# The table of expert groups in three pieces among the products of the last shared expert

## What is computed

```
x = x + layernorm(attention_block(layernorm(x)))
x = x + layernorm(experts(layernorm(x)))

# experts, E = 8 routed experts of inner width I = 176, top 2, shared expert of inner width SI = 704
shared  = (silu(x @ sw_gate) * (x @ sw_up)) @ sw_down
probs   = softmax(x @ router_w.T)
top_w, top_i = top_k(probs, 2);  top_w = top_w / sum(top_w)
h       = silu(x @ w_gate[e]) * (x @ w_up[e])          # for each expert e
routed  = sum over e of (h @ w_down[e]) * weight of e for the token
out     = routed + sigmoid(x @ shared_gate_w) * shared
```

## Time and profile before

| | us |
|---|---|
| median of 3 runs | 630.02 (627.61 to 630.73) |
| the profiled execution | 628.59 |
| its span, from the first to the last instruction | 626.9 |
| TensorE busy | 532.7 (85%) |
| VectorE busy | 413.1 (66%) |
| ScalarE busy | 259.0 (41%) |
| GpSimd busy | 110.3 (18%) |
| mean granted clock of TensorE | 0.922 |

### The profile page before, as it was taken

How to read it: one execution, slowest core, us unless ns; L and a number is a source line. 1 busy time by engine, 2 the same in 40 slices (tenths; PEclk the granted TensorE clock), 3 DMA queues, 4 the chain that set the end, 5 groups by cost and what they waited for, 6 DMA issues and landing times.

```text
span 626.9 us, 8174 instructions
## 1 busy us (share of the span) xinstructions
PE 532.7 (85%) x2464; PEld 421.3 (67%) x2464; DVE 413.1 (66%) x1249; ACT 259.0 (41%) x463; POOL 110.3 (18%) x133
## 2 busy tenths in 40 slices
PE   2835359999658999999989998999996989999991
PEld 1413235587437677787758886888784889999870
DVE  6786643779874698885488684333647747667447
ACT  3711344524355424357431444311232546666404
POOL 1510001300001404001205000031005014444400
PEclk9986678999767999999989999799987989999997
DMA  8970000001010003002001000010007214444273
GB/s 288 425 189 11 23 2 0 0 1 35 28 40 1 0 2 102 1 34 68 1 0 51 19 35 34 2 42 27 33 2 269 52 41 123 136 121 121 81 264 134
DMA packets 29549, 44.42 MB, mean 71 GB/s; under 512 B 3211, under 2 KB 24203, under 8 KB 29163
## 3 DMA queue, kind: packets, MB, share of 16 engines
q1 hardware_dynamic: 24515, 32.95, 16.4%
q0 software_dynamic: 3408, 9.38, 4.0%
q10 hardware_dynamic: 1584, 1.57, 0.8%
HBM read 27.55 MB, written 16.34 MB: 70 GB/s over the span
## 4 chain that ended last, share of the span: by engine, by line
PE 55%; DVE 33%; ACT 6%; issue 3%; DMA 2%; POOL 0%; ACTq 0%; POOLq 0%; DVEq 0%; SPq 0%
PE psum L723 10%; PE psum L764 10%; PE psum L724 10%; PE psum L725 9%; PE psum L790 5%; PE psum L733 3%; PE psum L839 3%; DVE rt L999 2%; DVE rt L1000 2%; DVE SM L1322 2%; PE psum L931 1%; DVE XC L1196 1%; PE psum L914 1%; PE psum L825 1%; PE psum L961 1%
## 5 line engine op out<-in xcount | busy, mean ns | idle before, releaser
L633 ACT ACTIVATE SM<-psum 128x512 f32<-128x512 f32 (+1 forms) x56 | 33.1, 595 | 132.0 <-PE psum L725 106.5
L1322 DVE TENSOR_TENSOR SM<-SM,psum 128x512 f32<-128x512 f32 (+1 forms) x56 | 38.1, 683 | 60.1 <-ACT SM L633 59.9
L509 POOL DMA_INDIRECT x_dispatched<-XN,dest x32 | 33.4, 1044 | 164.9 <-DVE XN L1390 156.3
L764 PE MATMUL psum<-WOU,SM 128*128 128x256 f32 x256 | 60.2, 379 | 0.2 <-DVE SM L1322 0.2
L790 PE MATMUL psum<-WQKV,HT 128*128 128x512 f32 (+1 forms) x128 | 51.1, 552 | 6.8 <-ACT GA L620 3.3
L500 POOL TENSOR_TENSOR OG<-QKV,hvec 128x256 f32<-128x256 f32 x16 | 13.3, 834 | 244.5 <-ACT IG L575 225.4
L764 PEld LDWEIGHTS psum<-WOU,SM 128*128 128x128 f32 x256 | 48.1, 189 | 9.2 <-issue 1.0
L518 POOL DMA_INDIRECT y_routed<-GO,g_dest x39 | 37.8, 969 | 70.1 <-ACT GO L698 69.8
L790 PEld LDWEIGHTS psum<-WQKV,HT 128*128 128x128 f32 x128 | 26.6, 213 | 29.7 <-issue 25.0
L764 PE MATMUL psum<-SDN,SM 128*128 128x256 f32 (+1 forms) x192 | 46.4, 392 | 0.1
L764 PEld LDWEIGHTS psum<-SDN,SM 128*128 128x128 f32 (+1 forms) x192 | 36.9, 195 | 7.7 <-issue 1.3
(11 more groups left out here) (285 smaller groups left out, 1357.1 us busy)
## 6 DMA issues: line engine op xcount, KB each, us to landing
XG<-x_dispatched SPq DMA_DIRECT2D x39, 130.0 KB, 2.6
YF<-y_routed SPq DMA_DIRECT2D x4, 1024.0 KB, 8.9
RUPR<-rup SPq DMA_DIRECT2D x1, 2816.0 KB
X<-x SPq DMA_DIRECT2D x4, 512.0 KB, 6.4
x_after_attention<-X SPq DMA_DIRECT2D x4, 512.0 KB, 2.8
QKV<-x ACTq DMA_DIRECT2D x3, 512.0 KB, 3.6
y_shared<-SH SPq DMA_DIRECT2D x3, 512.0 KB, 2.9
SHF<-y_shared SPq DMA_DIRECT2D x1, 1536.0 KB, 11.0
```

Of the source, the lines that this page charges most:

```text
L509: nc.gpsimd.indirect_dma_start(XD[:, :], bass.IndirectOffsetOnAxis(dest[:, i, old + j:old + j + 1], 0), XN[:, j, :], None).then_inc(dispat ...
L633: nc.scalar.activation(SM[0:rows, g % 3, 0:tb], p_pair(n)[0][0:rows, 0:tb], ACT.Silu).then_inc(silu_ready, 1)
L764: last = nc.tensor.matmul(p_down[:, j // 2, (j % 2) * D:(j % 2 + 1) * D], SM[0:rows, g % 3, j * P:(j + 1) * P], weight[0:rows, m, :], star ...
L1322: nc.vector.tensor_tensor(SM[0:rows, g % 3, 0:tb], SM[0:rows, g % 3, 0:tb], value_rows(n, rows)[:, 0:tb], ALU.mult).then_inc(hid_ready, 1)
```

## The change

The table gets steps of its own in the list, in three pieces: `("table", 3, 0)`, the limits of the experts (seven instructions, with a wait for the last of them added behind), `("table", 3, 1)`, the rows of the groups (L1140 to L1153, up to `table_ready`), and `("table", 3, 2)`, the spare rows (L1155 to L1160). The first two stand behind chunk 0 (`hid` 3,0), the third behind chunk 1 (`hid` 3,1) with `rsplit` 0. The other `rsplit` steps follow: 1 and 2 behind chunk 2, 3 and 4 behind chunk 3, 5 and 6 behind chunk 4, 7 behind chunk 5. GpSimd's row in `PLACE` is changed only in places that belong to steps in which GpSimd does nothing.

```diff
-    pieces = {1: [0, 1], 2: [2, 3], 3: [4, 5], 4: [6, 7]}
-    return order + weave(shared(b), {i: [("rsplit", b, m) for m in ms] for i, ms in pieces.items()})
+    tail = {0: [("table", b, 0), ("table", b, 1)], 1: [("table", b, 2), ("rsplit", b, 0)], 2: [("rsplit", b, 1), ("rsplit", b, 2)],
+            3: [("rsplit", b, 3), ("rsplit", b, 4)], 4: [("rsplit", b, 5), ("rsplit", b, 6)], 5: [("rsplit", b, 7)]}
+    return order + weave(shared(b), tail)
...
-            def table():
+            def per_slot(ap):
+                return ap.unsqueeze(1).broadcast_to([P, NG, E])
+            def table(m):
+                if m == 0:
+                    dve.wait_ge(hid_ready, SLOT[("rank", NB - 1, 0)] + 1)
+                    expert_limits()
+                if m == 1:
+                    group_rows()
+                if m == 2:
+                    spare_rows()
+            def expert_limits():
                 step(nc.vector.tensor_tensor(ntile_i[:, :], base[:, NB, :], base0[:, :], ALU.subtract))
...
                 step(nc.vector.tensor_tensor(jump[:, 1, :], lim[:, 1:E + 1], lim[:, 0:E], ALU.subtract))
-                def per_slot(ap):
-                    return ap.unsqueeze(1).broadcast_to([P, NG, E])
+                settle()
+            def group_rows():
                 link(nc.vector.tensor_tensor(past[:, :, :], slot_i[:, :].unsqueeze(2).broadcast_to([P, NG, E]), per_slot(ends[:, :]),
...
                 nc.vector.tensor_scalar(g_exp[:, :], g_exp[:, :], -1.0, float(E), ALU.mult, ALU.add).then_inc(table_ready, 1)
+            def spare_rows():
                 step(nc.vector.tensor_tensor(g_keep[:, :], g_row[:, :], g_lim[:, :], ALU.subtract))
...
                     nc.vector.reciprocal(gate[:, b % 2, 0:nj], top[:, 0, 0:nj]).then_inc(shared_gate, 1)
-                    if b == NB - 1:
-                        settle()
-                        dve.wait_ge(hid_ready, SLOT[("rank", b, 0)] + 1)
-                        table()
+                if stage == "table":
+                    settle()
+                    table(m)
```

## The result

The changed kernel takes 622.61 us in the median of four runs (621.20 to 623.98) against 629.96 before: ratio 0.9889, 95% interval 0.9851 to 0.9928. Two later sets of runs gave 0.9891 (0.9869 to 0.9912) and 0.9877 (0.9855 to 0.9899). The profiled execution took 623.98 us.

What follows compares the result with a forecast made beforehand. VectorE's queue order was taken as the bound: the table held up the product TensorE waited for. Terms 3.30 + 2.14 - 1.70 = 3.74 us off the median 630.02 gave 626.3 us; range 623.4 to 628.5.

Steps and rivals of the forecast that it cites:

- The stall: TensorE's wait for VectorE's product in the last shared expert: 5.85 us becomes 2.55, saving 3.30 us.
- The splits: VectorE's eight weight splits, moved later in the last shared expert: cost 0, with margins of 1.2 to 2.0 us.
- The other waiters: Group loads on SyncE's queue and GpSimd's scatters: scatters unchanged, first load still issued at about 486.5, cost 0.
- C: Rival: VectorE's splits become the bound ahead of the first group; at twice their length 635.7 us; chance 0.03.
- D: Rival: `hid` 3,2 waits for something other than product 0, so gain 0, 630.0 us; chance 0.03.
- A sign that came true by luck: TensorE's first transposes of a group at about 499 instead of 502.80, or at 497 if the clock stays up.
- case A: Rival: the clock stays up through the shorter stall before `hid` 3,3; gain 5.44 us, 624.6 us; chance 0.20.
- The old stall's clock: TensorE's half-speed stretch of 4.7 us at the stall before `hid` 3,2: 2.14 us lost, now saved.
- The new stall's clock: One half-speed stretch of 3.4 us at the shorter gap before `hid` 3,3: 1.70 us lost, 0 as other end.
- The entry to the groups: TensorE's 1.89 us gap before 505.35, ahead of the experts' groups: stays, with its slow stretch, so no gain.

Runs made afterwards that it cites:

- splits_only: Against the kernel before: only the splits moved back (one, two, two, two, one), the table left whole ahead of product 0; 629.73 us, ratio 1.0004.
- table_only: Against the changed kernel: splits put back two each behind chunks 1 to 4, so only the table is moved; 622.64 us, ratio 0.9892.
- one_piece_each: Against the changed kernel: one table piece behind each of `hid` 3,0, 3,1 and 3,2, the splits rearranged behind chunks 2 to 5; 624.11 us, ratio 0.9917.
- shift_4: Against the changed kernel: four dense products added on TensorE ahead of the last `rank`, pushing the stage back 0.93 us; 625.97 us, ratio 0.9947.
- shift_12: Against the changed kernel: twelve dense products added on TensorE ahead of the last `rank`, pushing the stage back 2.8 us; 628.41 us, ratio 0.9974.
- early_splits: Against the changed kernel: one table piece behind each of `hid` 3,0 to 3,2, splits 0 and 1 in VectorE's earlier wait; 621.84 us, ratio 0.9873.
- early_copies: Against early_splits: ScalarE's gate products of the last `shout` issued behind its first two copies of groups; 618.62 us, ratio 0.9817.
- whole_behind_0: Against the changed kernel: all three table pieces behind `hid` 3,0, ahead of product 1; 627.35 us, ratio 0.9966.
- after_again: The changed kernel itself, unaltered, with a second profile and five more rounds; 622.54 us, ratio 0.9891.
- after_third: The changed kernel itself, unaltered, profiled and timed again beside three others on the same chip; 622.01 us, ratio 0.9877.

## Why the prediction was wrong

*The stall.* It was right in place and size: 5.68 to 2.32 us, 3.36 saved where 3.30 was worked out. Limits, group rows and product 1 started 0.58, 1.85 and 5.96 us behind product 0, where the working had 0.60, 1.85 and 5.96. The limits with their added wait took 1.27 us for 1.25 worked out.

*The splits.* Right: cost 0, shown by splits_only and table_only. The margins that were worked out, 1.2 us for product 5 and 2.0 for split 7, are there in VectorE's timeline of the changed kernel:

```profile
495.67 0.69 DVE L1340 TENSOR_TENSOR SM<-SM,psum 64x512 f32<-64x512 f32 x1
496.28 1.22 DVE L1231 TENSOR_TENSOR RDNL<-RDNR,RDNH 88x1024 fp32r<-88x1024 f32 x1
```

Product 5 ended at 496.36, and `sdn` 3,5 began at about 497.7 (an estimate: eight products of 0.225 us ahead of 499.51); split 7 ended at 497.50, TensorE's products at 499.51. That these are small is what one_piece_each showed, with TensorE 2.3 us earlier.

*The other waiters.* One thing that was to show the prediction wrong did occur: the loads of the groups were issued later. The first came at 490.76, 19.9 us behind `hid` 3,0 where 17.8 was the distance before, behind GpSimd's last scatter issue, which took 2.96 us. The prediction had the scatters unchanged. It cost nothing, since TensorE's first group stood only at 499.51, and no row of TensorE's has a wait for a load there. C and D didn't occur.

*A sign that came true by luck.* The first transposes of a group were to stand at about 499, or at 497 in case A, and stood at 499.51. But `hid` 3,0 itself began 2.19 us later in this execution. Counted from there it is 28.68 us, and the prediction's two values are 30.4 and 28.4, so it is case A's.

*The old stall's clock.* Right: of the 5.48 us gained in the stage 3.36 are the gap's, and 2.12 are left for the clock, where 2.14 was worked out.

*The new stall's clock: the term that failed first.* The prediction took 1.70 us lost, "as both clean gaps had it", and gave 0 as the other end. It measured 0. The fault was to take two gaps of 2.05 and 1.89 us for a rule on the length of a gap. shift_4 and shift_12 show the same gap of 2.33 us with and without a slow stretch by its place, with stages 1.56 us apart (30.24 and 28.68). This is rival A, given 0.20 and priced at a gain of 5.44; the stage gained 5.48. The rule that spoke for A, from the Trainium skill's page "TensorE: Matmul & The Clock Gate" (HAM oscillation — how this bites in real kernels), warns only of longer idle gaps. It fits the changed kernel, but not shift_4, where a gap of 2.33 us did cost the clock.

*The entry to the groups: the term that failed second.* "The gap of 1.89 us before 505.35, at the entry to the groups, stays, with its slow stretch" was half right. The gap stayed, 1.89 us to the hundredth; the slow stretch went. It was worth 1.4 us. No rival had this; the prediction gave no reason why the slow stretch should stay when the gap moves. The stage ahead became 5.5 us shorter, so the entry came to lie elsewhere. That this decided is borne out by early_splits, where a still shorter stage brought the slow stretch back for 1.3 us, and by the shifted kernels.

With both terms at their measured values the sum is 3.30 + 2.14 + 1.4 = 6.8 us, and 6.9 was measured from `hid` 3,0 on. The first median, 7.35 us below, is 0.4 us more, which is within the spread of the times. Rival A alone would have given 624.6 us; the entry's 1.4 us brought the time below the range.

*What stays open.* I have shown that the place of a gap decides, not by what rule. In the changed kernel and the one before the clock's last rise came 4.1 to 4.3 us ahead of `hid` 3,0 in every profile of either kernel, and the outcome was the same in all of them; what ties the two together wasn't tried. For shift_12's entry the expectation built on fixed moments failed. Why only some executions have the slow stretch at 299 to 303 us is open too.

## What to carry to other kernels

A serial piece of small instructions (here 6.5 us on VectorE) belongs behind the operation that another engine waits for, in parts no longer than that engine's next chunk of work, as long as what stands behind it still comes in time (in one_piece_each it didn't). Here the shorter stall could be worked out from start times in two timelines to 0.1 us. A gap of some 2 us on TensorE had a second price, of 0, of 1.2 to 1.6 us, or once of 2.4 (the entry of shift_12), that depends on where it lies, and a change anywhere ahead can switch that price on or off at a later gap. So hold both values open for every gap behind the edit, not only for the one edited. Shortening gaps makes the time lower, as early_copies shows, and the entry's gap of 0.80 us was clean in both kernels that had it. That a gap is short is no warrant, though, as the third point below shows.

## What the runs showed of the hardware

- The same gap of 2.33 us between dense products left the granted clock at 1.00 (2.4 GHz) in two places (the changed kernel, shift_12) and was followed by 3.4 us at 0.50 (1.2 GHz) in a third (shift_4), 0.9 us away from the one and 1.9 us from the other. In shift_4 the clock fell at 481.04, 0.87 us after the gap had ended and dense work had begun again.
- A slow stretch of 3.4 us cost 1.2 us (the entry of whole_behind_0) to 1.6 (its stall; 1.55 in shift_4), not the 1.7 of half its length.
- A gap of 0.67 us before 586.05 was followed by a slow stretch (586.17 to 589.58) in the changed kernel's profile, and one of 0.66 us by a like one in early_copies (from 580.8) and in one_piece_each, but the gaps of 0.79 us in after_again and 0.66 us in after_third were not. It cost about 0.1 us there: without it TensorE waits 1.16 us for a DMA (`YF`) a little later (after_again).
- GpSimd's scatter issues took 0.97 us each (one 1.12), but the last two of the changed kernel took 1.70 and 2.96 us; they overlap with VectorE's splits of 482.82 to 487.7, which kept their 1.62 and 1.22. These two rows of GpSimd's timeline show it:

```profile
483.59 1.70 POOL L510 DMA_INDIRECT x_dispatched<-XN,dest  x1 [0.31 <-issue]
485.59 2.96 POOL L510 DMA_INDIRECT x_dispatched<-XN,dest  x1 [0.30 <-issue]
```

The cause wasn't tried by itself, but the other profiles speak for the splits. In one_piece_each and in early_splits, where the splits stand elsewhere, the last issue took 1.69 us and the one ahead of it, begun before any split, 0.97. In splits_only only one issue began during a split, and took 1.61. Over all fourteen profiles the 21 issues begun during a split took 1.56 to 2.97 us; of the 91 others one took 2.96 (in table_only, with a split starting 0.5 us into it) and the rest at most 1.13. The loads behind the scatters were issued 2.1 us later than before against the stage; they still came 8.7 us ahead of the first group's transposes, which hid it.
